# Half-row projections between the scores, in a fused attention and expert block on one core

## The reference

```python
h = _layernorm(x) * (1 + ca) + sa
qkv = h @ w_qkv.T + b_qkv            # 16 heads of 16
scores = q @ k.T / 4 + causal_alibi  # -(q-k) for k <= q, else -1e30
out = (softmax(scores) @ v) @ w_out.T + b_out
x = x + ga * out
h = _layernorm(x) * (1 + cb) + sb
p = softmax(h @ gate_W.T)            # 8 experts
# per token: cnt[e] = how many of the 0/1 values (p > 0.3) equal e
# final = sum over e of (h @ expert_W[e].T) * cnt[e] * p[e]
x = x + gb * (final @ out_W.T)
```

## Time and profile before

| | |
|---|---|
| median of three runs | 1565.01 us |
| profiled execution: span | 1560.2 us (its own time outside the span isn't listed; the runs' median is 4.8 us above) |
| TensorE / VectorE / ScalarE / POOL busy | 94 / 82 / 74 / 55 % |
| mean granted TensorE clock | 0.983 of full |
| DMA | 239.73 MB, 154 GB/s |
| chain that ended last | PE 62%, DVE 10%, DMA 9%, issue 6%, SP's queue 6% |

### The profile page before, as it was taken

One profiled execution on the slowest core, in us unless ns is written; L12 is line 12 of the kernel. 1 busy time (PEld: TensorE's weight loads), 2 busy tenths in 40 slices (PEclk: granted clock), 3 DMA queues, 4 the chain that ended last, 5 costly groups with the idle time before them and its releaser, 6 DMA issues.

```text
span 1560.2 us, 56229 instructions
## 1 busy us (share of the span) xinstructions
PE 1472.0 (94%) x21476; PEld 946.3 (61%) x21476; DVE 1277.9 (82%) x3030; ACT 1147.2 (74%) x2464; POOL 858.0 (55%) x924
## 2 busy tenths in 40 slices
PE   6888999999999999999999999999999999999996
PEld 5555656666666666666666666656666656666653
DVE  6777888888888888888888888888888888888836
ACT  2477777778777777777877877777777777777762
POOL 2124556556556556655655665565665565566454
PEclk9799999999999999999999999999999999999988
DMA  5344555555455555455555545555545555554521
GB/s 170 99 150 127 171 156 173 152 170 157 149 178 155 175 153 166 143 168 167 157 180 152 160 146 170 166 160 157 165 142 167 175 150 178 154 169 139 157 73 50
DMA packets 197298, 239.73 MB, mean 154 GB/s; under 512 B 22462, under 2 KB 147782, under 8 KB 197030
## 3 DMA queue, kind: packets, MB, share of 16 engines
q1 hardware_dynamic: 196972, 236.07, 49.4%
q10 hardware_dynamic: 64, 0.07, 0.0%
HBM read 134.25 MB, written 100.73 MB: 151 GB/s over the span
## 4 chain that ended last, share of the span: by engine, by line
PE 62%; DVE 10%; DMA 9%; issue 6%; SPq 6%; ACT 3%; POOL 2%; POOLq 0%; DVEq 0%; ACTq 0%
PE ps L599 26%; PE ps L753 11%; PE ps L748 8%; PE ps L807 6%; DMA qk_d<-qk_st 5%; PE ps L802 5%; DVE mxp L1089 3%; DMA kz<-qk_d 2%; PE ps L768 2%; PE ps L662 2%; SPq L412 2%; DVE ve_c L1014 1%; DVE zr L1101 1%; DVE st_c L1000 1%; SPq L429 1%
## 5 line engine op out<-in xcount | busy, mean ns | idle before, releaser
L1089 DVE TENSOR_REDUCE mxp<-ps 128x4 f32<-128x512 f32 (+1 forms) x1536 | 842.8, 592 | 160.5 <-PE ps L768 155.6
L863 ACT ACTIVATE prob<-ps 128x512 f32<-128x512 f32 (+1 forms) x1536 | 732.6, 525 | 121.8 <-PE ps L753 116.4
L753 PE MATMUL ps<-qs,kz 50*128 50x128 f16 (+2 forms) x3584 | 405.9, 240 | 12.9 <-DVE mxp L1089 10.5
L768 PE MATMUL ps<-kz,qs 49*128 49x128 f16 (+1 forms) x4096 | 410.5, 231 | 0.1
L753 PEld LDWEIGHTS ps<-qs,kz 50*128 50x128 f16 x3584 | 261.4, 94 | 88.7 <-ACT prob L863 31.1
L768 PEld LDWEIGHTS ps<-kz,qs 49*128 49x128 f16 x4096 | 286.3, 95 | 3.8 <-DVE mxp L1089 1.8
L1347 POOL TENSOR_TENSOR om<-oc,rz 128x512 f32<-128x512 f32 x62 | 77.4, 1270 | 329.9 <-DMA rz<-rz_d 329.9
L807 PE MATMUL ps<-prob,va 128*32 128x384 f32 (+2 forms) x3072 | 237.6, 381 | 0.0
L748 PE MATMUL ps<-mk 64*128 64x256 bf16 x1024 | 198.6, 274 | 36.0 <-DMA kz<-qk_d 11.3
L802 PE MATMUL ps<-prob,va 128*32 128x128 f32 x4096 | 209.6, 277 | 0.6 <-DVE qk_st L1021 0.6
L764 PE MATMUL ps<-mk 64*128 64x256 bf16 x1024 | 201.0, 276 | 5.4 <-DVE mxp L1089 3.4
(11 more groups left out here) (157 smaller groups left out, 2870.6 us busy)
## 6 DMA issues: line engine op xcount, KB each, us to landing
qk_d<-qk_st SPq DMA_DIRECT2D x128, 256.0 KB, 2.8
ou_d<-ou SPq DMA_DIRECT2D x124, 256.0 KB, 2.3
qs<-qk_d SPq DMA_DIRECT2D x256, 96.0 KB, 2.4
kz<-qk_d SPq DMA_DIRECT2D x256, 96.0 KB, 2.5
xa<-in_L_attn_x SPq DMA_DIRECT2D x32, 512.0 KB, 5.2
qk_d<-qk_st SPq DMA_DIRECT2D x128, 128.0 KB, 3.4
xc<-in_L_attn_x SPq DMA_DIRECT2D x32, 512.0 KB, 4.1
oc<-ou_d SPq DMA_DIRECT2D x31, 512.0 KB, 4.9
```

Source lines behind the costliest of these rows:

```text
L753: x_ = mm(bank[:, col:col + w * P], kz[rows, h // 2, kt * P:(kt + 1) * P], qs[rows, h // 2, qt * P:(qt + w) * P], start=(n > 0), stop=(n > ...
L768: x_ = mm(bank[:, col * P:(col + w) * P], qs[rows, h // 2, qt * P:(qt + 1) * P], kz[rows, h // 2, kt * P:(kt + w) * P], start=(n > 0), sto ...
L863: nc.scalar.activation(prob[:, h % 8, at:at + w], ps[:, ST + n, 0:w], ACT.Exp, scale=1.0 / FS).then_inc(s["exp_done"], 1)
L1089: v.tensor_reduce(mxp[:, g % 2, at, first:first + apart * (BLOCKS[n] - 1) + 1:apart], bank.rearrange("p (m k) -> p m k", k=P), AX.X, ALU.m ...
```

## The change

- **Half passes in pieces.** The tables are now by gap: a slot's three chunks are three gaps, 48 in an iteration. The 12 projections form a ring, `CHAIN`. Each is cut into passes on rows 0 to 63 and on rows 64 to 127. The lower rows of one are issued in turn with the upper rows of the one before it in the ring, into different banks, in three gaps, two of six steps in each.
- **Transposes** `ta`, `t2` and `mt` also go in two halves of 64 rows, the second behind a wait for the first.
- **PSUM.** Two banks for scores, two for row scores, taken in turn over the chunks; PE waits for the reader two chunks back. Four banks (4 to 7) are for the rest.
- **Low halves.** ScalarE writes `qk_f` (fp32) and the high half; POOL subtracts. `hh_a` and `hh_c` become a copy by POOL from `hf`; `ve` goes to POOL, `nm` falls away.
- **Order.** `ta` and its followers are one iteration earlier, `norm_c`, x1 (now two buffers) and others move, SP's list is new; `z0` 3, `zs` 2 and 3 and the last `finish` and store fall in a third iteration. All lists for the end go.

```diff
+CHAIN = [("qk", 0, 1, (0, 1, 2)), ("qk", 1, 1, (3, 5, 6)), ("qk", 2, 1, (7, 8, 9)),
+         ("v", 0, 1, (10, 13, 15)), ("qk", 3, 1, (17, 18, 19)), ("v", 1, 1, (21, 22, 24)),
+         ("moe", 0, -2, (25, 26, 27)), ("moe", 1, -2, (28, 29, 31)), ("out", 0, -1, (34, 35, 36)),
+         ("out", 1, -1, (37, 39, 40)), ("moe", 2, -2, (41, 42, 43)), ("moe", 3, -2, (45, 46, 47))]
 PE_AT = {
+    2: [("mt", 1, 0)], 3: [("mt_hi", 1, 0)], 5: [("pv", 3, -1)], 11: [("t2", 0, -2), ("t2_hi", 0, -2), ("t2", 1, -2)],
+    12: [("t2_hi", 1, -2)], 16: [("mt", 2, 0)], 17: [("mt_hi", 2, 0)], 20: [("pv", 0, 0)], 23: [("gate", 0, -2)],
+    25: [("ta", 0, 2), ("ta_hi", 0, 2)], 30: [("mt", 3, 0), ("mt_hi", 3, 0)], 32: [("pv", 1, 0)],
+    38: [("ta", 1, 2), ("ta_hi", 1, 2)], 41: [("mt", 0, 1)], 42: [("mt_hi", 0, 1)], 44: [("pv", 2, 0)],
 }
 ACT_AT = {
+    2: [("z0", 3, -3)], 3: [("negm", 1, 0)], 5: [("ou", 3, -1)], 6: [("qk_hi", 0, 1)], 9: [("qk_hi", 1, 1)],
+    11: [("hf_c", 0, -2)], 15: [("hf_c", 1, -2)], 18: [("negm", 2, 0)], 19: [("qk_hi", 2, 1)], 20: [("vst", 0, 1)],
+    22: [("ou", 0, 0)], 24: [("gate_exp", 0, -2), ("qk_hi", 3, 1)], 27: [("hf_a", 0, 2)],
+    30: [("negm", 3, 0), ("oh", 0, -1)], 31: [("oh", 1, -1), ("z0", 0, -2)], 32: [("vst", 1, 1)], 36: [("ou", 1, 0)],
+    37: [("z0", 1, -2)], 38: [("hf_a", 1, 2)], 42: [("negm", 0, 1)], 44: [("ou", 2, 0)], 47: [("z0", 2, -2)],
 }
 DVE_AT = {
+    0: [("zs", 2, -3), ("rmax", 1, 0)], 3: [("bn_c", 2, -2), ("bn_c", 3, -2), ("ag_c", 0, -2)], 4: [("bn_a", 3, 2)],
+    5: [("ag_a", 0, 2), ("zs", 3, -3)], 7: [("set_b", 0, 1)], 12: [("set_w", 0, 1)], 15: [("set_e", 0, 1), ("rmax", 2, 0)],
+    18: [("invert", 0, -1)], 23: [("gate_max", 0, -2)], 24: [("gate_sum", 0, -2)], 25: [("rmax", 3, 0)],
+    27: [("gate_p", 0, -2)], 29: [("gate_count", 0, -2)], 30: [("gate_scale", 0, -2), ("bn_a", 0, 3)], 32: [("zs", 0, -2)],
+    36: [("rmax", 0, 1), ("bn_a", 1, 3)], 39: [("zs", 1, -2)], 42: [("bn_a", 2, 3)], 43: [("ot", 0, -1)],
+    44: [("ot", 1, -1), ("bn_c", 0, -1)], 45: [("bn_c", 1, -1)],
 }
 POOL_AT = {
+    0: [("norm_c", 0, -2), ("norm_a", 0, 2)], 2: [("qk_lo", 0, 1)], 5: [("qk_lo", 1, 1), ("finish", 1, -3)],
+    7: [("hh_c", 0, -2), ("spread", 2, 0)], 8: [("hh_c", 1, -2)], 10: [("spread", 3, 0), ("hl_c", 0, -2)],
+    12: [("hl_c", 1, -2)], 16: [("qk_lo", 2, 1)], 17: [("om", 0, -1)], 19: [("om", 1, -1)],
+    22: [("ol", 0, -1), ("ol", 1, -1)], 25: [("xg", 0, -1)], 26: [("hh_a", 0, 2)], 31: [("qk_lo", 3, 1)],
+    37: [("hl_a", 0, 2), ("spread", 0, 1)], 39: [("x1", 0, -1)], 43: [("hh_a", 1, 2), ("hl_a", 1, 2), ("x1", 1, -1)],
+    45: [("finish", 0, -2)], 46: [("spread", 1, 1)],
 }
 SP_AT = {
+    1: [("load_aug", 1, 0), ("store_ou", 2, -1)], 8: [("load_z", 0, -1)], 14: [("store_qk", 0, 1), ("load_a", 0, 3)],
+    16: [("load_o", 0, -1)], 17: [("store_qk", 1, 1)], 18: [("load_aug", 2, 0), ("load_stack", 0, 1)],
+    20: [("load_c", 0, -1)], 22: [("store_rz", 0, -1), ("load_rz", 0, -1)], 24: [("store_qk", 2, 1)],
+    25: [("store_ou", 0, 0), ("load_gb", 0, -2)], 26: [("load_aug", 3, 0)], 27: [("store_res", 0, -3)],
+    32: [("load_stack", 1, 1)], 36: [("store_qk", 3, 1)], 37: [("load_aug", 0, 1)],
+    38: [("load_stack", 2, 1), ("load_stack", 3, 1)], 43: [("store_ou", 1, 0), ("load_ga", 0, 0)], 47: [("store_ou", 3, 0)],
 }
+ST, MX = (0, 1), (2, 3)
...
+                for g in range(2 * place, 2 * place + 2):
+                    for u in range(2):
+                        if live(pb) and u < PIECES[pname]:
+                            last = g == 5 and u == PIECES[pname] - 1
+                            x_ = halves[pname][0](ps[:, BANK[pname, pn], :], pn, 1, g // 3, g % 3, u, False, last)
+                            if last:
+                                x_.then_inc(s[halves[pname][2]], 1)
+                        if live(b) and u < PIECES[name]:
+                            x_ = halves[name][0](ps[:, BANK[name, n], :], n, 0, g // 3, g % 3, u, (g, u) == (0, 0), False)
+                            if (g, u) == (5, PIECES[name] - 1):
+                                x_.then_inc(s["half_done"], 1)
...
-                    wait(pe, "exp_done", i * 48 + 3 * t + n - 2)
+                    wait(pe, "exp_done", i * 48 + 3 * t + n - 1)
...
-                    wait(pe, "mx_read", bm * 48 + 3 * pos + n - 2)
+                    wait(pe, "mx_read", bm * 48 + 3 * pos + n - 1)
...
+                nc.scalar.activation(qk_f[:, k, :], ps[:, BANK["qk", n], :], ACT.Identity,
+                                     bias=bqk[:, 2 * k + n // 2:2 * k + n // 2 + 1]).then_inc(s["qk_full"], 1)
...
+            def qk_lo(b, n):
+
+                wait(pool, "qk_full", b * 4 + n + 1)
+                wait(pool, "qk_hi", b * 4 + n + 1)
+                q.tensor_tensor(qk_st[:, n % 2, 1, :], qk_f[:, n % 2, :], qk_st[:, n % 2, 0, :],
+                                ALU.subtract).then_inc(s["qk_lo"], 1)
```

More of the change, by code:

```diff
@@ L52 @@
[L52 to L62, removed]
@@ L110 @@
 HALF = 64
+PIECES = {"qk": 1, "v": 2, "out": 2, "moe": 1}
+ST, MX = (0, 1), (2, 3)
 PARTS = 48
@@ L311, in bank_of, with iterations, play @@
-        def bank_of(name, n, b):
-            return TAIL[name, n, b][0] if (name, n, b) in TAIL else MISC + BANK[name, n]
         def live(b):
             return 0 <= b < NB
-        def iterations(eng, one, drain=None, end=0):
-            for i in range(-2, NB + end if drain else NB + 2):
+        def iterations(one):
+            for i in range(-2, NB + 3):
                 one(i)
-            if drain:
-                drain()
         early = ("load_a", "bn_a", "ag_a", "norm_a")
-        def play(i, t, table, steps, part=None, late={}):
-            for place in range(4):
-                for at, name, n, off in table.get(t, []):
-                    if at == place and live(i + off) and not (name in early and i + off == 0):
+        def play(i, table, steps, part=None, late={}):
+            for gap in range(GAPS):
+                for name, n, off in table.get(gap, []):
+                    if live(i + off) and not (name in early and i + off == 0):
@@ L331, in play @@
                         steps[name](i + off, n)
-                    elif at == place and i + off == -2 and (name, n) in late:
+                    elif i + off == -2 and (name, n) in late:
                         late[name, n]()
-                if part is not None and place < 3:
-                    part(i, t, place)
-        SIDE = [(t, name, n, off) for t in range(SLOTS) for at, name, n, off in sorted(PE_AT.get(t, []), key=lambda x: x[0])]
+                if part is not None:
+                    part(i, gap)
@@ L538, in one @@
             def one(i):
-                for t in range(SLOTS):
-                    play(i, t, SP_END if i == PRE else SP_AT, steps)
-            iterations(sp, one, drain, -1)
-            wait(sp, "res_stored", (NB + 1) * 16)
+                play(i, SP_AT, steps)
+            iterations(one)
+            wait(sp, "res_stored", NB * 16)
         @block.tensor
@@ new lines, in mt_hi, with qk @@
+            def mt_hi(b, n):
+                dst = ps[:, BANK["mt", n], :]
+                wait(pe, "mt_half", b * 4 + n + 1)
+                nc.tensor.transpose(dst[:, HALF:P], mxt[HALF:P, n, :], ident[HALF:P, HALF:P]).then_inc(s["mt_ready"], 1)
+            def qk(dst, n, j, c, m, u, first, last):
+                rows = slice(HALF * j, HALF * j + HALF)
+                w, h = ((wqkv_hi, hh_a), (wqkv_hi, hl_a), (wqkv_lo, hh_a))[m]
+                col = (n % 2) * D + (n // 2) * P
+                return mm(dst, w[rows, c, col:col + P], h[rows, c, :], start=first, stop=last)
```

659 lines of the change are left out of this document (177 added, 482 removed), and 13 rows, old and new, of the table PE_AT.

## The result

The changed kernel takes 1899.31 us (median of 4 runs, 1897.73 to 1904.99) against 1566.06 us before (4 runs, 1564.07 to 1570.75): a ratio of 1.213, interval 1.2104 to 1.2156. The forecast was 1544 us. Its profiled span is 1896.3 us.

The account below looks back on a forecast made before the run. TensorE, 94% busy, was taken as the bound. Start 56 + 32 x 44.4 + tail 62 = 1538.8 us of span, plus 4.8 for the runs' median, gave 1544 us; 8-in-10 range 1488 to 1608, likeliest case 1509 to 1563.

Parts of the forecast that it names:

- POOL's sum and the walk built on it: POOL's work per batch about 35 us, 27 before; gap-by-gap walk of its list, norms 3.2 to 10.4 us after gap 0.
- the queues, +0.8: Waits in POOL's and SP's lists for rz, om and stack 2: net +0.8 us per batch, bounds 0 and 3.
- Fewer switches, halves side by side: TensorE's 64-row half passes overlap and save 13 switches to 128 rows: -2.5 us a batch, floor 40.5 us.
- D: Rival: TensorE's half passes don't overlap, 15.5 us more per batch, over 2000 us; chance 0.02.
- Two banks, +2.3: TensorE waits for ACT and DVE with two banks instead of three: +2.3 us per batch, bounds 0 and 4.
- Rival B: Two banks for scores and maxima cost twice the forecast's sum: period 45.8 us, 1589 us; chance 0.14.
- Low halves on POOL: Four qk_lo move from DVE to POOL: 4.5 us more POOL work per batch; DVE loses 4 x 0.66.
- POOL copies at 0.66: POOL's four fp16 copies of 512 elements taken at 0.66 us each, 2.6 per batch; upper bound 1.16.
- Rival C: POOL's order becomes the bound, PE waits for hl and stack 2: period 46.7 us, 1617 us; chance 0.19.
- Start and tail: Outside the loop: start +3 us (0 to 8) to 56; tail +17 (10 to 25), 62 for 45.
- The period of 44.4: Loop time per batch: 40.5 + 0.8 + 2.3 + 0.8 = 44.4 us, 1.3 less than 45.7.

Follow-up runs that it names:

- e1_add: Changed kernel with POOL's normalise back as add and multiply, using a negated mean that POOL makes: 1754.12 us, ratio 1.1186.
- e15_order_only: Same lists as e14_whole_rz, but POOL's slow subtract form kept, against the changed kernel: period 51.40 us; the form is worth 146 us here.
- e14_whole_rz: e12_add_sp_a with the reciprocal six gaps earlier, store_rz and load_rz ahead of the large loads, load_a after load_o: 109 us less, period 47.03 us.
- e12_add_sp_a: Changed kernel with add form, stack 0's stores and loads ahead of SyncE's large loads, load_a directly behind stack 0: 109 us above e14_whole_rz.
- e16_whole_s1: e14_whole_rz with stack 1's loads at gap 24 for 32: 1599 us, ratio interval 1.0166 to 1.0221 against the kernel before.
- e5_two_banks: Kernel before with only scores and row maxima alternating over two banks each instead of three: +451 us, 13.9 us per batch.
- e17: Like e16_whole_s1, but low halves on VectorE from PSUM, without the fp32 copy and POOL's subtractions: 1603 us.
- e7_dve_lo: Changed kernel with low halves of queries and keys back on VectorE, slow normalise and SP's order kept: 65 us less than the changed kernel.
- e11_half_alone_a: Like e12_add_sp_a (add form, SyncE's list reordered), but low halves on VectorE from PSUM: period 51.2 us.

## Why the prediction was wrong, step by step

In short: the mechanism forecast for TensorE came, and what failed is the walk through the lists of POOL and SyncE that feed it. The order in which they deliver was priced at +0.8 us per batch; in the runs the slow form and the lists together cost 9.0.

- **The step that failed: POOL's sum and the walk built on it ("norm_c and norm_a 3.2 to 10.4 us after gap 0", queues +0.8).** I took the normalise at its old 559 ns and counted of its rewriting only the small `ve` steps. It runs at 1223: 8 x 0.66 = 5.3 us more of POOL per batch, at the head of the list on which the stores hang. Laid on the batch shown (the norms began at 3.2 in the walk and at 895.62 in the trace, so its zero is 892.4), they end at 15.8 for 10.4, the first store leaves at 16.9 for 11.6: late by the 5.3. That is 4.2 us of period by `e1_add` (55.02 to 50.83) and 4.4 by `e15_order_only` against `e14_whole_rz` (51.40 to 47.03). The full diff of the kernels showed the new operation (what is printed of it above does not) and no row had its duration; there I set no bounds. That the cost goes by the place and not by POOL's sum rests on ScalarE's wait for the store (98.8 and 90.8 us with the form, 5.9 and 4.2 without) and on POOL, which is busy for only 1198 of the loop's 1760 us; no run has the form in the changed kernel at another place with SyncE's list mended.
- **The second part of the same step: the queues, +0.8 with bounds 0 and 3.** With the form mended the lists still cost 50.83 - 46.00 = 4.8 us of period. From the first store to the load of stack 0 the walk has 5.4 us (11.6 to 17), the trace 9.0 (909.34 to 918.33): it left out the loads of `xa` and `oc`, which stand between the two pairs of stores (in `e14_whole_rz`, which has them behind, this stretch takes 4.2 us). So `store_rz` is at 28.2 for 19.8 and `om` at 36.6 for 28; the 8.3 us between these two were right. Nor did it have ScalarE's `qk_hi` 2 waiting for the store of pair 0. It saw `om` at 28 and `oh` at 27.4 and priced that at nearly nothing; moving the reciprocal, its store and its load (and `load_a` behind them) took 3.5 us (`e12_add_sp_a` to `e14_whole_rz`).
- **The clock** was in no step of the loop. 0.91 over the loop for 0.99, and 0.50 for about 12 us in the batch shown. In these runs it came and went with the holes: in `e16_whole_s1` the loop's clock is 0.99 again. What part of the period is the clock's was not separated.
- *Fewer switches, halves side by side* (floor 40.5): the mechanism is right by the timeline, and D is out; the floor itself was not measured.
- *Two banks, +2.3*: about right for the changed order as far as the waits show; no run has the half passes with three banks. The ten rows of the view of waits in which PE or its weight loads wait for exps or maxima add up to 186.5 us in `e16_whole_s1` against 128.6 before, 1.8 us per batch more. Rival B is then too high for this order and, with `e5_two_banks` at +13.9 per batch, far too small for the old one.
- *Low halves on POOL*: nothing in the final lists (`e16` and `e17`, 1599 and 1603), 2.1 us of period in the changed kernel as it is (`e7_dve_lo`): a cost of place, not of work.
- *POOL copies at 0.66*: 0.61. The 769 ns that the Trainium skill's GPSIMD Engine Reference (3.1) gives for a tight loop over 512 elements is higher than this case's row of 610 ns.
- *Rival C* (POOL's order is the bound) comes nearest, at 46.7 us; 55.0 was measured. It too had the normalise at 559, worth 4.2 us, and it had PE waiting for `hl` and stack 2, where the trace shows stack 0 (`kz<-qk_d`, 109.0 us) and exps that stand behind ScalarE's wait.
- *Start and tail*: 65.5 for 56 and 70.3 for 62. The form is not the tail's miss, since `e14_whole_rz` with the old form has 69.5; which of its steps is, stays open. As listed, the prediction's terms of the tail add up to 59.1 us, not 62 (61.6 if the overlap of 2.5 is not taken off).
- The period of 44.4 was not reached: of the 10.6 us missed, 4.2 are the form and 4.8 the lists, and the 1.6 by which `e16_whole_s1` (46.0) is above it are not assigned. So with form and lists mended as far as tried the change still doesn't pay: 9 us in the loop, 9 in the start, 25 in the tail.

## What to carry to other kernels

When a diff swaps an operation's arithmetic (add to subtract) treat it as a new instruction with an unknown price, even when shape, types and engine stay. When work moves to the head of an in-order list, walk every list that hangs on it, entry by entry, with each entry's wait: a slack that the list shows further down is not there for its head. And when several mendings end at the same time, look for the hole in the trace before blaming a shared resource: the next late operand stands where the last one stood.

## What the runs showed of the hardware

- POOL, 128x256 fp32 with two per-partition scalars: add then multiply 558 ns, subtract then multiply 1223 to 1227 ns, whatever the stride of the scalar.
- TensorE's clock: in the changed kernel PE's starts leave some 8 us of holes between 911.4 and 922.3, the granted clock is 0.50 (1.2 GHz) in the windows from 916 to 928 and 1.00 from 932. In `e11_half_alone_a` PE is busy for 1.46 us of 912 to 916, and the clock is 0.50 from 916 to 920 and 0.96 from 920. At 0.50 two pairs of half passes start 0.43 us apart, at 1.00 0.22.
- Two matmul passes of 512 columns on 64 rows each, on different halves of the rows and in different banks, start within 0.02 us and cost the time of one (0.22 us to the next pair).
- Two banks for three groups per slot that stand together: +451 us, 13.9 us per batch (`e5_two_banks`). With other matmuls between the groups the waits for exps and maxima are 1.8 us per batch above those with three (`e16_whole_s1`), by the view of waits.
- A store of 256 and one of 128 KB (`qk_st`) issued behind loads of 1 MB: 5.3 us until SyncE could go on in the batch shown; at most 2.3 us in `e14_whole_rz`, without those loads.
